# Three weight products as one VectorE instruction over three PSUM banks, two query products as one over two

## The chip, the cores and the metric

The kernel runs on one core of a Trainium2 chip. The metric is the time of one launch in device microseconds (us), the median of several runs. A second figure, the span, is read from one profiled execution: from its first to its last instruction.

## The reference, cut to what matters

One decoder layer over x of 32 x 64 x 512 (2048 rows of 512), in three stages, each followed by a layer norm over 512:

1. x = LN(x + A(x)), with A a small network of four layers on 64 channels (a scan along the sequence and a feed forward of 64 to 256 to 64), projected from 512 and back to 512.
2. x = LN(x + AC(x, ctx, ctx)), the autocorrelation attention. For each of 8 heads and each channel: corr = ifft(fft(q) * conj(fft(k))) over 64 positions, the 8 largest lags, a softmax over them, and a weighted sum of v shifted by these lags (positions clamped to the last one).
3. x = LN(x + FF(x)), with x and weight fake-quantized in blocks of 32 to a 4-bit format, one 512 x 512 product and a bias.

In the kernel the transforms of stage 2 are products with constant matrices. A complex product in the frequency domain is three real products of sums ("forms"), and 96 rows of them hold 32 frequencies of one sequence. The forms of ctx are computed once and kept in SBUF (`ctxf`, three chunks of 512 columns for each tile: sequence 0, sequence 1, and a rest chunk with what is left of both).

## The kernel before, in words

The 2048 rows are 16 tiles of 128 rows (`PAIRS`, each two sequences of 64). All five engines have an instruction stream written out by hand, and semaphores order them. The first part, `slot_loop`, is stage 1. Then comes a software pipeline of 22 turns (`for t in range(1, PAIRS + LAG)`, with LAG = 7) in which every engine works once on up to seven tiles at different stages. One turn of VectorE, in its order (lines 1177 to 1193), for the tile number in brackets: `top_sum` (t-3), `fed` (t-7), `attended` (t), `weight_products` (t-4), `block_scales` (t-5), `without_largest` (t-3), `largest` (t-2), `crossed` (t-4), `rounding` (t-5), `query_products` (t-1).

Those that matter here:

- `query_products` (L1053): two multiplications of 96 partitions x 512, banks 5 and 6 of PSUM (`query_forms`, L376) by `ctxf`, into PQ. `correlation` (L387) on TensorE needs both.
- `weight_products` (L1095): three multiplications of 128 x 512. The first is of bank 7 (`weight_rest_forms`, L411), the other two of banks 5 and 6 (`weight_forms`, L419). TensorE's `out_rest` (L429) reads the first result and `out_even` (L436) the other two.
- Banks 5 and 6 are used in turn by query forms and weight forms: L419 waits until the query products have been read out (`s_pq`), and L376 until the weight products have been (`s_pw`).
- The two matmuls of L419 use 64 rows each, on different halves of the array, and so do those of L376.
- `block_scales` (`scales`, L999 a reduction, L1001 and L1002 tensor_scalar on 128 x 16, L1003 a reciprocal), then `without_largest` (L1083, eight match_replace). L1083 releases GpSimd's `chosen` (L852), which releases TensorE's transposes `weights_to_time` (L401), then ScalarE's copy (L639), then L411 and L419.
- `rounding` (`magic`, L1007 and L1008) releases GpSimd's `clamped` (L858, L859), behind which stand in GpSimd's order `differences` (L841 to L843), `rounded_off` (L865 and the dequantization L754), `finished` (L875) and, in the next turn, `scaled` (L749) and `chosen` (L852).
- TensorE's order in a turn: feed forward (L461, L464), L401, projection (L363), L411, L419, L387, L429, L376, L444, L436.

Of the kernel before, what the change touches and what calls it, by code (L numbers as in the profile page):

```python
# [6 lines left out]
ALU = mybir.AluOpType  # L7
# [8 lines left out]
L = 64  # L16
# [6 lines left out]
PAIRS = ROWS // P  # L23
HC = ROWS // 2
SEQ = HC // L
N = 512
# [9 lines left out]
EVEN = 96  # L36
# [113 lines left out]
def build(nc, xT, x, ctx_in, consts_in, winT, w1T, w2T, woutT, cols, wq_in, rows, out):  # L150
    with ExitStack() as stack:
        def sb(name, shape, dt=F32):
            return stack.enter_context(nc.sbuf_tensor(name, shape, dt))
# [4 lines left out]
        ps = stack.enter_context(nc.psum_tensor("ps", [P, 8 * N], F32))  # L158

        def bank(b):  # L160
            return ps[:, b * N:(b + 1) * N]


        ctxf = sb("ctxf", [P, PAIRS * 3 * N])
# [32 lines left out]
        def piece(k, n=1):  # L197
            return big[:, k * N:(k + n) * N]
# [11 lines left out]
        PQ = piece(0, 2)  # L210
# [1 line left out]
        REST, G, PART, WN, WT = (piece(4 + k) for k in range(5))  # L212
        part = ctxf[0:SPLIT, (3 * PAIRS - 2) * N:(3 * PAIRS - 1) * N].bitcast(BF16)
        bias3 = win_sb[0:SPLIT, :].bitcast(BF16)
        PW = [piece(9 + k) for k in range(3)]
        JUNK = [piece(12), piece(13), PART]

        def mat(k):
            return consts[:, k * P:(k + 1) * P]
# [34 lines left out]
        def row(n):  # L254
            return X[:, bass.ts(n, N)]
# [16 lines left out]
        def here(n):  # L272

            return 0 <= n < PAIRS
# [61 lines left out]
        def _(pe):  # L336
            mm = nc.tensor.matmul
# [6 lines left out]
            for cc in range(2):  # L344
                for g in range(2):
                    pe.wait_ge(s_xt[2 * cc + g], 16)
                for c in range(VC):
                    for g in range(2):
                        last = mm(ps[g * D:(g + 1) * D, cc * N:(cc + 1) * N], win_sb[:, c * D:(c + 1) * D],  # L349
                                  piece(4 * (2 * cc + g) + c), start=(c == 0), stop=(c == VC - 1))  # L350
# [15 lines left out]
            def query_forms(n):  # L366

                if here(n):
                    pe.wait_ge(s_ln[0], n + 1)
                    for b in range(2):  # L370
                        if n >= 3:
                            pe.wait_ge(s_pw, 3 * n - 7 + b)
                        elif n >= 1:
                            pe.wait_ge(s_pq, 2 * n - 1 + b)
                        half = slice(b * L, (b + 1) * L)
                        mm(bank(5 + b)[0:EVEN, :], mat(XQ_A)[half, 0:EVEN], row(n)[half, :], start=True, stop=True  # L376
                           ).then_inc(s_q, 1)

            def correlation(n):

                if here(n):
                    pe.wait_ge(s_pq, 2 * n + 2)
                    if n >= 1:
                        pe.wait_ge(s_ce, n)
                    for j in range(VC):
                        for b in range(2):
                            last = mm(ps[:, 2 * N + j * P + b * L:2 * N + j * P + (b + 1) * L],  # L387
                                      PQ[0:EVEN, b * N + j * P:b * N + (j + 1) * P], mat(IC_E)[0:EVEN, 0:L],
                                      start=True, stop=True)
                    last.then_inc(s_c, 1)  # L390
# [14 lines left out]
            def weight_rest_forms(n):  # L405

                if here(n):
                    pe.wait_ge(s_wte, n + 1)
                    if n >= 1:
                        pe.wait_ge(s_pw, 3 * n - 2)  # L410
                    mm(bank(7), mat(XW_C), WT, start=True, stop=True).then_inc(s_w, 1)  # L411

            def weight_forms(n):

                if here(n):
                    for b in range(2):
                        pe.wait_ge(s_pq, min(2 * n + 5 + b, 2 * PAIRS))
                        half = slice(b * L, (b + 1) * L)
                        mm(bank(5 + b), mat(XW_A)[half, :], WT[half, :], start=True, stop=True).then_inc(s_w, 1)  # L419

            def out_rest(n):

                if here(n):
                    pe.wait_ge(s_pw, 3 * n + 1)
                    if n == 0:
                        pe.wait_ge(s_rs1, SLOTS + 2)
                    if n >= 1:
                        pe.wait_ge(s_sum[1], n)
                    mm(bank(4), mat(OI_C), PW[0], start=True, stop=False, skip_group_check=True)  # L429

            def out_even(n):

                if here(n):
                    for b in range(2):
                        pe.wait_ge(s_pw, 3 * n + 2 + b)
                        last = mm(bank(4)[b * L:(b + 1) * L, :], mat(OI_A)[:, 0:L], PW[1 + b], start=False,  # L436
                                  stop=True, skip_group_check=True)
                    last.then_inc(s_o, 1)

# [28 lines left out]
            def slot(m, l, s, first, second):  # L468
# [32 lines left out]
                for q in range(4):  # L501
                    if second:
                        if q == 0:
                            pe.wait_ge(s_xn2, m)
                        if early and q == 2:
                            query_forms(0)
                        if early and q >= 2:
                            pe.wait_ge(s_act, 4 * m + q - 5)
                        mm(hb[q], w1z[:, q * P:(q + 1) * P], XN[o], start=True, stop=True).then_inc(s_hidmm, 1)  # L509
                context(3)  # L510
                context(4)
                if early:
                    correlation(0)
                    projection(1)
# [13 lines left out]
            for t in range(1, PAIRS + LAG):  # L528
                feed_forward(t - 7)
                weights_to_time(t - 4)  # L530
                if t >= 2:
                    projection(t)
                weight_rest_forms(t - 4)
                weight_forms(t - 4)
                if t >= 3:
                    correlation(t - 2)
                out_rest(t - 4)
                if t >= 2:
                    query_forms(t - 1)
                if t == 1:  # L540
                    pe.wait_ge(s_sq1, SLOTS + 2)
                    mm(bank(4), mat(MEAN), SQ_LAST, start=True, stop=True).then_inc(s_var1, 1)
                quantized_to_channels(t - 6)
                out_even(t - 4)
# [346 lines left out]
        def _(dve):  # L891
            v_ = nc.vector
            tt, ts, stt = v_.tensor_tensor, v_.tensor_scalar, v_.scalar_tensor_tensor
# [151 lines left out]
            def query_products(n):  # L1045

                if here(n):
                    for b in range(2):
                        dve.wait_ge(s_q, 2 * n + b + 1)
                        if n >= 1:  # L1050
                            dve.wait_ge(s_c, n)
                        at = (3 * n + b) * N
                        tt(PQ[0:EVEN, b * N:(b + 1) * N], bank(5 + b)[0:EVEN, :], ctxf[0:EVEN, at:at + N], ALU.mult  # L1053
                           ).then_inc(s_pq, 1)

            def largest(n):

# [29 lines left out]
            def weight_products(n):  # L1087

                if here(n):
                    for b, (to, chunk) in enumerate(((7, 2), (5, 0), (6, 1))):  # L1090
                        dve.wait_ge(s_w, 3 * n + b + 1)
                        if n >= 1:
                            dve.wait_ge(s_o, n)
                        at = (3 * n + chunk) * N
                        tt(PW[b], bank(to), ctxf[:, at:at + N], ALU.mult).then_inc(s_pw, 1)  # L1095

            def block_scales(n):

# [18 lines left out]
            def slot(m, l, s, first, second):  # L1117
# [25 lines left out]
                if early:  # L1143
                    attended(0)
                    query_products(0)
                    largest(0)
# [30 lines left out]
            for t in range(1, PAIRS + LAG):  # L1177
                top_sum(t - 3)
                fed(t - 7)
                attended(t)  # L1180
                weight_products(t - 4)
                block_scales(t - 5)
                without_largest(t - 3)
                if t >= 3:
                    largest(t - 2)
                crossed(t - 4)
                rounding(t - 5)
                if t == 1:
                    dve.wait_ge(s_mlp, SLOTS)
                    ts(H[:, N:2 * N], XC[1], curm[:, B2:B2 + 1], None, ALU.add).then_inc(s_h, 1)  # L1190
                    last_norm(1, RS_LAST)
                if t >= 2:
                    query_products(t - 1)
# [42 lines left out]
```

## Time and profile before

| | us |
|---|---|
| median of 3 runs | 364.13 (363.85 to 365.54) |
| the profiled execution's own time | 364.46 |
| its span | 362.5 |
| VectorE busy | 274.7 (76%) |
| TensorE busy | 295.6 (82%) |
| GpSimd busy | 184.3 (51%) |
| L1095, weight products, 48 instructions | 30.7 |
| L1053, query products, 32 instructions | 20.5 |

The turns of the pipeline lie between about 151 and 360 us of the span. Each engine's busy time is a mean over the whole span, so a share says little on which of them sets the length of a turn. Of a matmul the end is modelled. In the timeline instructions of one line that follow each other are merged: "x3" and 1.88 us are three instructions from the start of the first to the end of the last.

### The profile page before, as it was taken

The numbers are of one execution on the slowest core, as the hardware profiler recorded it, in microseconds if no ns is written. First come the engines' busy times: TensorE is split into PE (matmuls) and PEld (weight loads), VectorE is DVE, ScalarE is ACT, GpSimd is POOL, SyncE is SP. The second block draws the span as 40 slices with busy tenths as digits, with TensorE's granted clock in tenths as the row PEclk, the third lists the DMA queues.
The fourth block names the chain that finished last, engine by engine and source line by source line (L and its number), as shares of the span: only waits on it lengthen the run. The fifth ranks groups of instructions, "written<-read, shape, count | busy, mean of one in ns | idle before, by whom it ended". The sixth has DMA issues, their size and how long they took to land.

```text
span 362.5 us, 4947 instructions
## 1 busy us (share of the span) xinstructions
PE 295.6 (82%) x1071; PEld 122.9 (34%) x1080; DVE 274.7 (76%) x927; ACT 252.0 (70%) x586; POOL 184.3 (51%) x213
## 2 busy tenths in 40 slices
PE   1578589889899898796599999999999998986633
PEld 1222233333333333241344444433444443332100
DVE  6748695967768578514659999999999999987730
ACT  4028288888988888676647788777879777664722
POOL 1008961041040113100333888888898888988782
PEclk9987699999999999989889999999999999998955
DMA  6999049731021100540000000000000000000002
GB/s 210 393 309 361 32 80 181 146 102 29 0 72 29 29 14 0 155 78 0 1 0 2 2 1 1 31 30 29 32 30 28 5 30 29 31 30 29 30 29 87
DMA packets 14413, 24.53 MB, mean 68 GB/s; under 512 B 2611, under 2 KB 3251, under 8 KB 14390
## 3 DMA queue, kind: packets, MB, share of 16 engines
q1 hardware_dynamic: 12310, 20.09, 16.6%
q0 software_dynamic: 2080, 4.19, 6.9%
q8 instruction: 7, 0.11, 0.1%
q14 instruction: 16, 0.13, 0.1%
HBM read 15.89 MB, written 4.19 MB: 55 GB/s over the span
## 4 chain that ended last, share of the span: by engine, by line
PE 34%; DVE 30%; issue 12%; ACT 10%; POOL 9%; DMA 3%; SPq 1%; POOLq 0%; ACTq 0%; DVEq 0%
PE ps L509 8%; PE ps L477 6%; DVE X L1018 4%; DVE big L1083 4%; PE ps L522 4%; DVE big L1095 3%; DVE m L1064 3%; DMA big<-in_xT_dram 3%; PE ps L349 3%; DVE qa L1001 2%; PE ps L487 2%; DVE qa L999 2%; PE ps L411 2%; PE ps L387 2%; DVE big L1141 2%
## 5 line engine op out<-in xcount | busy, mean ns | idle before, releaser
L749 POOL TENSOR_TENSOR big<-X,qs 128x512 f32<-128x512 f32 x20 | 20.9, 1046 | 60.0 <-DVE qs L1003 59.9
L477 PE MATMUL ps<-ctx_ring,consts 128*128 128x512 f32 x96 | 50.1, 635 | 0.8 <-ACT ctxf L660 0.8
L570 ACT ACTIVATE big<-X,lnv 128x512 f32<-128x512 f32 x48 | 34.2, 712 | 9.6 <-DVE X L1018 9.6
L509 PE MATMUL ps<-big,w1z 128*128 128x512 f32 x64 | 31.4, 632 | 10.9 <-DVE big L1141 10.0
L1018 DVE SCALAR_TENSOR_TENSOR X<-ps,X 128x512 f32<-128x512 f32 x48 | 31.9, 679 | 10.8 <-PE ps L464 7.2
L1095 DVE TENSOR_TENSOR big<-ps,ctxf 128x512 f32<-128x512 f32 x48 | 30.7, 681 | 5.4 <-PE ps L411 3.7
L387 PEld LDWEIGHTS ps<-consts,big 96*128 96x128 f32 x256 | 29.9, 191 | 12.0 <-issue 11.1
L387 PE MATMUL ps<-consts,big 96*128 96x64 f32 x256 | 31.9, 278 | 0.1
L477 PEld LDWEIGHTS ps<-ctx_ring,consts 128*128 128x128 f32 x96 | 18.0, 200 | 30.2 <-ACT ctxf L660 15.8
L692 ACT ACTIVATE big<-ps,curm 128x512 f32<-128x512 f32 x32 | 22.0, 692 | 6.7 <-PE ps L509 6.7
L852 POOL TENSOR_TENSOR big<-big 128x512 f32<-128x512 f32 x16 | 20.3, 1269 | 11.7 <-DVE big L1083 11.6
L599 ACT ACTIVATE X<-X,lnv 128x512 f32<-128x512 f32 x32 | 24.7, 807 | 2.0
L1083 DVE MATCH_REPLACE8 big<-w,big 128x64 f32<-128x64 f32 x128 | 25.0, 208 | 0.1
L660 ACT ACTIVATE ctxf<-ps 128x512 f32 (+1 forms) x40 | 23.3, 594 | 0.7 <-PE ps L477 0.6
L1053 DVE TENSOR_TENSOR big<-ps,ctxf 96x512 f32<-96x512 f32 x32 | 20.5, 679 | 4.1 <-PE ps L376 4.1
L761 POOL TENSOR_SCALAR big<-big 128x512 f32<-128x512 f32 x4 | 2.5, 613 | 41.1 <-issue 41.0
L509 PEld LDWEIGHTS ps<-big,w1z 128*128 128x128 f32 x64 | 11.7, 194 | 29.8 <-issue 21.0
L754 POOL TENSOR_TENSOR xq<-big,qs 128x512 bf16<-128x512 f32 x20 | 21.0, 1050 | 1.6
L859 POOL TENSOR_TENSOR big<-big 128x512 f32<-128x512 f32 x16 | 20.3, 1268 | 1.3
L411 PE MATMUL ps<-big,consts 128*128 128x512 f32 x32 | 18.7, 667 | 2.7 <-ACT big L639 2.7
L1064 DVE MAX8 m<-big 128x8 f32<-128x64 f32 x128 | 17.6, 210 | 3.8 <-ACT big L608 3.8
L865 POOL TENSOR_TENSOR big<-big 128x512 f32<-128x512 f32 x16 | 20.4, 1272 | 0.2
(175 smaller groups left out, 695.9 us busy)
## 6 DMA issues: line engine op xcount, KB each, us to landing
big<-in_xT_dram SPq DMA_DIRECT2D x4, 1024.0 KB, 10.9
ctx_ring<-in_ctx_dram SPq DMA_DIRECT2D x16, 256.0 KB, 2.8
out_dram<-X SPq DMA_DIRECT2D x16, 256.0 KB, 2.0
X<-in_x_dram SPq DMA_DIRECT2D x2, 1536.0 KB, 12.7
X<-rows_sb POOLq DMA_DIRECT2D x1, 3072.0 KB, 22.0
X<-in_wq_dram SPq DMA_DIRECT2D x1, 1024.0 KB, 8.2
X<-in_x_dram SPq DMA_DIRECT2D x2, 512.0 KB, 4.0
X<-rows_sb POOLq DMA_DIRECT2D x1, 1024.0 KB, 8.0
```

The costliest lines, as they stand in the source:

```text
L387: last = mm(ps[:, 2 * N + j * P + b * L:2 * N + j * P + (b + 1) * L], PQ[0:EVEN, b * N + j * P:b * N + (j + 1) * P], mat(IC_E)[0:EVEN, 0:L ...
L411: mm(bank(7), mat(XW_C), WT, start=True, stop=True).then_inc(s_w, 1)
L477: mm(bank(6 + t % 2), mat((CY_0, CY_1, CY_C)[t % 3]), ctx_ring[:, r * N:(r + 1) * N], start=True, stop=True).then_inc(s_cform, 1)
L509: mm(hb[q], w1z[:, q * P:(q + 1) * P], XN[o], start=True, stop=True).then_inc(s_hidmm, 1)
L570: squared[k] = chain(a(JUNK[k], row(n), ACT.Square, bias=st[:, 0:1], scale=-float(V), accum_out=st[:, 2:3]))
L599: a(row(n), row(n), ACT.Identity, bias=st[:, 5:6], scale=st[:, 4:5]).then_inc(s_ln[k], 1)
L660: a(ctxf[:, bass.ts(6 * m + t, N)], bank(6 + t % 2), ACT.Copy).then_inc(s_fe, 1)
L692: a(hs[q], hb[q], ACT.Silu, bias=curm[:, B1_0 + q % 2:B1_0 + q % 2 + 1]).then_inc(s_act, 1)
L1018: stt(row(m), bank(b), 0.0, row(m), ALU.add, ALU.add, accum_out=st[:, 0:1]).then_inc(s_sum[k], 1)
L1064: last = v_.max(top[:, g * TOP:(g + 1) * TOP], CR[n % 2][:, g * L:(g + 1) * L])
L1083: last = v_.match_replace(REST[:, g * L:(g + 1) * L], w8[:, g * TOP:(g + 1) * TOP], G[:, g * L:(g + 1) * L], 0.0)
L1095: tt(PW[b], bank(to), ctxf[:, at:at + N], ALU.mult).then_inc(s_pw, 1)
```

## The change: what it does

The three multiplications become one of 128 x 1536 over banks 5, 6 and 7, the two become one of 96 x 1024 over banks 5 and 6. Results lie in the same SBUF columns, those of the rest chunk now last. Each of these instructions increments its semaphore once, so all waits on `s_pw` and `s_pq` count tiles and no longer pieces. The weight product now waits for all three forms (`s_w` at 3n+3), the query product for both (`s_q` at 2n+2). TensorE's waits follow: one for the whole product in place of one for each piece.

```diff
 def query_forms(n):
     pe.wait_ge(s_ln[0], n + 1)
+    if n >= 3:
+        pe.wait_ge(s_pw, n - 2)
+    elif n >= 1:
+        pe.wait_ge(s_pq, n)
     for b in range(2):
-        if n >= 3:
-            pe.wait_ge(s_pw, 3 * n - 7 + b)
-        elif n >= 1:
-            pe.wait_ge(s_pq, 2 * n - 1 + b)
...
 def correlation(n):
-    pe.wait_ge(s_pq, 2 * n + 2)
+    pe.wait_ge(s_pq, n + 1)
...
 def weight_rest_forms(n):
-    pe.wait_ge(s_pw, 3 * n - 2)
+    pe.wait_ge(s_pw, n)
...
 def weight_forms(n):
+    pe.wait_ge(s_pq, min(n + 3, PAIRS))
     for b in range(2):
-        pe.wait_ge(s_pq, min(2 * n + 5 + b, 2 * PAIRS))
...
 def out_rest(n):
-    pe.wait_ge(s_pw, 3 * n + 1)
+    pe.wait_ge(s_pw, n + 1)
-    mm(bank(4), mat(OI_C), PW[0], start=True, stop=False, skip_group_check=True)
+    mm(bank(4), mat(OI_C), piece(PW + 2), start=True, stop=False, skip_group_check=True)
...
 def out_even(n):
     for b in range(2):
-        pe.wait_ge(s_pw, 3 * n + 2 + b)
...
 def query_products(n):
-    for b in range(2):
-        dve.wait_ge(s_q, 2 * n + b + 1)
-        if n >= 1:
-            dve.wait_ge(s_c, n)
-        at = (3 * n + b) * N
-        tt(PQ[0:EVEN, b * N:(b + 1) * N], bank(5 + b)[0:EVEN, :], ctxf[0:EVEN, at:at + N], ALU.mult
-           ).then_inc(s_pq, 1)
+    dve.wait_ge(s_q, 2 * n + 2)
+    if n >= 1:
+        dve.wait_ge(s_c, n)
+    tt(PQ[0:EVEN, :], ps[0:EVEN, 5 * N:7 * N], ctxf[0:EVEN, 3 * n * N:(3 * n + 2) * N], ALU.mult
+       ).then_inc(s_pq, 1)
...
 def weight_products(n):
-    for b, (to, chunk) in enumerate(((7, 2), (5, 0), (6, 1))):
-        dve.wait_ge(s_w, 3 * n + b + 1)
-        if n >= 1:
-            dve.wait_ge(s_o, n)
-        at = (3 * n + chunk) * N
-        tt(PW[b], bank(to), ctxf[:, at:at + N], ALU.mult).then_inc(s_pw, 1)
+    dve.wait_ge(s_w, 3 * n + 3)
+    if n >= 1:
+        dve.wait_ge(s_o, n)
+    tt(piece(PW, 3), ps[:, 5 * N:8 * N], ctxf[:, 3 * n * N:3 * (n + 1) * N], ALU.mult
+       ).then_inc(s_pw, 1)
```

## Rows read from the trace of the kernel before

**Rows 1.** The page, busy us of each engine, share of the span, instructions.

```profile
PE 295.6 (82%) x1071; PEld 122.9 (34%) x1080; DVE 274.7 (76%) x927; ACT 252.0 (70%) x586; POOL 184.3 (51%) x213
```

**Rows 2.** Busy time in four stretches of one turn each, from 222.90 to 264.60.

```profile
sum 41.70, PE 39.78 PEld 17.80 DVE 41.15 ACT 33.89 POOL 35.66; mean PE 9.95 PEld 4.45 DVE 10.29 ACT 8.47 POOL 8.92
```

**Rows 3.** Timeline of a full turn: start, us, engine, line, count, idle time before.

```profile
261.70 0.43 DVE L1008 TENSOR_SCALAR big<-big 128x512 f32<-128x512 f32 x1
...
262.05 1.28 DVE L1053 TENSOR_TENSOR big<-ps,ctxf 96x512 f32<-96x512 f32 x2
...
263.52 1.13 PE L419 MATMUL ps<-big,consts 64*128 64x512 f32 x4
...
264.59 1.88 DVE L1095 TENSOR_TENSOR big<-ps,ctxf 128x512 f32<-128x512 f32 x3
...
266.39 0.67 DVE L999 TENSOR_REDUCE qa<-X 128x16 f32<-128x512 f32 x1
...
267.02 1.05 POOL L754 TENSOR_TENSOR xq<-big,qs 128x512 bf16<-128x512 f32 x1
267.09 1.01 DVE L1001 TENSOR_SCALAR qa<-qa 128x16 int32<-128x16 int32 x1
...
268.13 0.20 DVE L1002 TENSOR_SCALAR qs<-qa 128x16 f32<-128x16 f32 x1
```

**Rows 4.** Line 1001 over the whole span: ns min/median/max, first and last start.

```profile
L1001 DVE TENSOR_SCALAR qa<-qa x20: 174/390/1023, 27.5 to 343.9; 128x16 int32<-128x16 int32 x20
```

**Rows 5.** Groups of the page; and a timeline row with eight short VectorE instructions.

```profile
L1095 DVE TENSOR_TENSOR big<-ps,ctxf 128x512 f32<-128x512 f32 x48 | 30.7, 681 | 5.4 <-PE ps L411 3.7
...
L1053 DVE TENSOR_TENSOR big<-ps,ctxf 96x512 f32<-96x512 f32 x32 | 20.5, 679 | 4.1 <-PE ps L376 4.1
...
270.20 1.10 DVE L1064 MAX8 m<-big 128x8 f32<-128x64 f32 x8
```

**Rows 6.** Timeline of the first turns with weight products, 184 to 207 us.

```profile
188.83 1.27 POOL L852 TENSOR_TENSOR big<-big 128x512 f32<-128x512 f32 x1 [5.05 <-DVE big L1083]
...
190.69 0.66 PE L401 MATMUL ps<-consts,big 128*128 128x128 f32 x4
...
193.09 1.13 PE L419 MATMUL ps<-big,consts 64*128 64x512 f32 x4
...
194.25 1.29 DVE L1095 TENSOR_TENSOR big<-ps,ctxf 128x512 f32<-128x512 f32 x2 [0.21 <-PE ps L419]
...
196.38 0.17 DVE L1002 TENSOR_SCALAR qs<-qa 128x16 f32<-128x16 f32 x1
...
198.41 1.27 POOL L852 TENSOR_TENSOR big<-big 128x512 f32<-128x512 f32 x1 [0.45 <-DVE big L1083]
...
202.14 1.13 PE L419 MATMUL ps<-big,consts 64*128 64x512 f32 x4
...
202.60 1.99 DVE L1095 TENSOR_TENSOR big<-ps,ctxf 128x512 f32<-128x512 f32 x3
...
205.21 0.39 DVE L1001 TENSOR_SCALAR qa<-qa 128x16 int32<-128x16 int32 x1
...
205.64 0.17 DVE L1002 TENSOR_SCALAR qs<-qa 128x16 f32<-128x16 f32 x1
205.66 1.07 POOL L754 TENSOR_TENSOR xq<-big,qs 128x512 bf16<-128x512 f32 x1
```

**Rows 7.** Timeline of the last turns with weight products, 308 to 339 us.

```profile
308.84 0.18 DVE L1002 TENSOR_SCALAR qs<-qa 128x16 f32<-128x16 f32 x1
308.85 1.07 POOL L754 TENSOR_TENSOR xq<-big,qs 128x512 bf16<-128x512 f32 x1
...
311.65 1.26 POOL L852 TENSOR_TENSOR big<-big 128x512 f32<-128x512 f32 x1
...
316.52 1.29 DVE L1095 TENSOR_TENSOR big<-ps,ctxf 128x512 f32<-128x512 f32 x2 [0.34 <-PE ps L419]
...
337.23 1.29 DVE L1095 TENSOR_TENSOR big<-ps,ctxf 128x512 f32<-128x512 f32 x2 [0.36 <-PE ps L419]
```

More of the change, by code:

```diff
@@ L214, in build @@
         bias3 = win_sb[0:SPLIT, :].bitcast(BF16)
-        PW = [piece(9 + k) for k in range(3)]
+        PW = 9
         JUNK = [piece(12), piece(13), PART]
@@ L434, in out_even @@
                     for b in range(2):
-                        pe.wait_ge(s_pw, 3 * n + 2 + b)
-                        last = mm(bank(4)[b * L:(b + 1) * L, :], mat(OI_A)[:, 0:L], PW[1 + b], start=False,
+                        last = mm(bank(4)[b * L:(b + 1) * L, :], mat(OI_A)[:, 0:L], piece(PW + b), start=False,
                                   stop=True, skip_group_check=True)
```

## The prediction

> **What bounds the kernel now.** I read the page's busy shares first, then the busy time of single turns, then the timeline of one full turn, and last the timelines of the first and the last turns that have weight products. The page shows no engine full over the span [rows 1]. Four turns in the middle take 41.70 us, 10.42 each, and in them VectorE is busy 41.15 of 41.70, TensorE 39.78, GpSimd 35.66 [rows 2]. So VectorE looks like the bound there, and fewer instructions on it look like time won.
>
> The timeline of one turn says otherwise [rows 3]. L1001 works on 16 columns, and its shortest instances take 0.174 us [rows 4]. In this turn it takes 1.01: from 267.09 to 268.10, where GpSimd's L754, begun at 267.02, ends at 268.07. In the eight turns from 215 to 299 us I see the same: L754 starts 0.05 to 0.07 before L1001, and L1001 ends about 0.03 after it. Where VectorE came first, L1001 or L1002 took 0.17 to 0.39, as at 205.21 and 205.64 [rows 6]. So 0.8 us of VectorE's busy time in a full turn is waiting for GpSimd, and the turn is a loop of both: L1008 ends, GpSimd runs L858 to L754, L1001 ends 0.03 behind L754, then VectorE runs L1002, L1083, L1064 and so on to the next L1008. From the end of L1008 (262.13) to the end of L1001 (268.10) are 5.97 us, and the weight products lie inside these beside GpSimd's work [rows 3]. While L1001 loses that race, no saving in the products shortens a turn.
>
> **The price of an instruction.** Three products take 1.88 us with 0.68 for the last alone, a step of 0.60 [rows 3, 5]. Eight L1064 of 64 elements take 1.10 with 0.21 for the last, a step of 0.127 [rows 5]. A line through both gives 1.06 ns an element and 0.06 us an instruction. The trace has no instruction over several banks. The bounds of the fixed part are 0 (three products still cost 1.80) and 0.127 (a whole short instruction; they cost 1.55). A step from bank to bank could cost something too, but nothing in rows prices it. I take 0.06, since it accounts for both steps: the weight product 1.68 instead of 1.80, the query product 1.14 instead of 1.20. Over 16 tiles these are 16 x 0.18 = 2.9 us of VectorE time.
>
> The Trainium skill ("Perfetto Trace Analysis", Optimizing Scalar/DVE Operations) gives a larger estimate, about 125 ns of data access per VectorE instruction from PSUM, and advises larger operations for a saturated engine. By it the weight product saves 0.25 us a turn, not 0.12. The same section advises the reverse, breaking up instructions, where an engine is not saturated and others wait for it, and that is the case of the first and last turns below.
>
> **What the merged wait costs.** The merged product needs both L419 forms. The two matmuls run side by side, so waiting for the second costs nothing; what is lost is the first product (bank 7), which now waits as well. A product that waited for L419 started 1.16 after it: 193.09 to 194.25 [rows 6]. In a full turn that is 263.52 + 1.16 = 264.68, where before the first one started at 264.59. The merged one ends its step at 264.68 + 1.68 = 266.36, against 266.39. L1001 is then ready at 267.06, 0.03 earlier than before, but L754 starts at 267.02 as ever [rows 3]: it still loses, by 0.04. The query product ends near 263.2 and L419 starts at 263.52 behind L411, so that wait stays covered. TensorE's L429 and L376 now wait for all products (about 266.45); L429 follows L387 at about the same time, and TensorE has 10.42 - 9.95 = 0.47 us free in a turn [rows 2]. So the full turns stay at 10.42: term 0.
>
> **The first turns.** Here VectorE waits for L419 and the first product was ahead of it. The weight products then end 1.68 instead of 1.21 (two steps of 0.60) after the release: +0.47 us a turn. Turn by turn:
> - The turn at 185 us: L852 moves from 188.83 to 189.30 and ends at 190.57; L401 starts at 190.69 behind other matmuls [rows 6]. Hidden.
> - The turn at 194: +0.47, and L852 at 198.41 had waited for L1083, so it, L401 and L419 at 202.14 move by 0.47 [rows 6].
> - The turn at 203: L419 at 202.61, product from 203.77 to 205.45, L1001 ready at 206.16. L754, which hangs on L1008 and so moves by 0.47 as well, starts at 206.13. Before, L1001 and L1002 got in ahead of it (205.21, 205.64). Now L1001 loses by 0.03, ends at 206.13 + 1.05 + 0.03 = 207.21, and L1002 starts at 207.24 instead of 205.64: +1.60 [rows 6].
> The loop then carries 1.60 through the full turns.
>
> **The last turns.**
> - At 308, where before L1002 (308.84) got in ahead of L754 (308.85), the same geometry makes L1001 lose: L1002 at 309.96, 1.12 later. From L1002 to L852 are 2.03 (196.38 to 198.41), so L852 comes at 311.99; before, it stood at 311.65, not waiting for VectorE: +0.34 [rows 6, 7].
> - At 316.52 the products waited for L419: +0.47 again, 0.81 in all [rows 7].
> - At 326 the delay is largely hidden, since the chain goes through GpSimd. At 337.23 it is +0.47: 1.28 in all [rows 7].
>
> Sum: 1.60 + 0 + 1.28 = 2.9 us. Against the profiled execution's own time, 364.46 (span 362.5), that is 367.4; this execution is 0.33 over the median of the runs, so 367.0 for the median. If the delays of both ends are half covered, it is 365.6. With the product at 1.80, L1001 loses by more and each edge turn pays 0.12 more, some 0.5 in all: 367.5. With 1.55, L1001 is ready at 266.93, ahead of L754, which is the first rival.
>
> **Rivals.**
> 1. *The race is won.* L1001 gets in ahead of L754 at 205, in full turns and at 308. A win gives VectorE 0.8 us, but TensorE's chain L401 to L419 does not follow at once, so I expect a win in every second turn, about 0.4 a turn, with TensorE's 0.47 as the cap. Nine turns give 3.5 us; the edges still cost 0.47 three or four times, 1.7. Time 364.1 - 3.5 + 1.7 = 362.3. For it: the margin is only 0.04 and the true step may be 1.60 to 1.65. Against it: L1001 lost at 0.05 late, and L1002 won only when it started ahead (205.64 against 205.66). Chance 0.16. By the page's 125 ns the margin would turn to 0.09 in favour.
> 2. *VectorE is the plain bound* and the waits are covered: the 2.9 us are won, 361.2. For it: 10.29 busy of 10.42. Against it: L1001's 1.01. Chance 0.08.
> 3. *The edges absorb it.* The full turns gain nothing, and most of the delays of the first and last turns fall beside GpSimd or TensorE work: 364.1 to 365.9. For it: the turn at 185 and the one at 326 hide theirs. Chance 0.22.
> 4. *The product over banks is slower than three* (over 1.80), or TensorE starves behind the late L429: beyond 368.3. Chance 0.06.
> The forecast itself has 0.48, with its own range of 366.0 to 368.3.
>
> **How the numbers follow.** A measurement of this kernel tells about 0.5% from no change, 1.8 us: faster is below 362.3, slower above 365.95. Slower: 0.48 + 0.06 + a little of rival 3, 0.56. Faster: half of rival 1 and rival 2, with what lies near the edge, 0.16. Same: 0.28. The range leaves out rival 2 and the upper tail and reaches into rival 1: 362.4 to 368.3.
>
> **What would show each step.** In the profile after: a weight product of about 1.75 us (step 1.68) that starts 1.16 after L419 in every turn, with idle VectorE ahead of it in full turns too; the full turn still 10.42; L1001 at 1.01 in all full turns, and now also at the two places near 206 and 309. The forecast is wrong if L1001 is short in the full turns (rival 1), if the full turn falls to about 10.2 with VectorE unbroken (rival 2), or if L419 of the turn at 212 us is late by much less than 1.6 (rival 3).

## The result and the profile after

The changed kernel takes 369.24 us (median of 4 runs, 367.99 to 370.39), the kernel before 364.84 beside it (4 runs). The ratio is 1.0118, with a 95% interval of 1.0064 to 1.0172: slower, by about 4.4 us. I had forecast 367.0 within 362.4 to 368.3, a loss of 2.9 us. The direction was right, the loss was forecast 1.5 us too small, and the time lies outside the range. Measured once more in six runs the ratio was 1.0154 (1.0118 to 1.0190), 5.6 us between the medians. Executions more than 1.5% over the fastest of their kernel stay out of the ratios: two of the twelve with the query products alone (366.03 and 366.92), and one of the kernel before (382.93).

The two profiled executions differ by 3.5 us in span (362.5 and 366.0), but the changed one happened to reach the pipeline 1.6 us sooner: the first L851, which was L852 before, starts at 177.38 against 178.96. (The page's lines have shifted by up to five: L1090 is now the weight product, L1050 the query product, L1000 and L1001 the two tensor_scalar, L1007 was L1008, L753, L851, L864 and L874 were L754, L852, L865 and L875.) The next fences are timeline rows (start, us, engine, line, count, idle time before), first of the changed kernel: the first, fourth and thirteenth L851, the last one, and the last L874.

```profile
177.38 1.27 POOL L851 TENSOR_TENSOR big<-big 128x512 f32<-128x512 f32 x1 [2.65 <-DVE big L1080]
...
208.00 1.27 POOL L851 TENSOR_TENSOR big<-big 128x512 f32<-128x512 f32 x1 [0.38 <-DVE big L1080]
...
301.81 1.27 POOL L851 TENSOR_TENSOR big<-big 128x512 f32<-128x512 f32 x1 [0.36 <-DVE big L1080]
...
333.07 1.27 POOL L851 TENSOR_TENSOR big<-big 128x512 f32<-128x512 f32 x1 [0.36 <-DVE big L1080]
...
362.81 0.77 POOL L874 TENSOR_SCALAR X<-X,lnv 128x512 f32<-128x512 f32 x1 [2.98 <-ACT lnv L578]
```

The same instructions before:

```profile
178.96 1.27 POOL L852 TENSOR_TENSOR big<-big 128x512 f32<-128x512 f32 x1 [2.65 <-DVE big L1083]
...
207.81 1.27 POOL L852 TENSOR_TENSOR big<-big 128x512 f32<-128x512 f32 x1
...
301.62 1.27 POOL L852 TENSOR_TENSOR big<-big 128x512 f32<-128x512 f32 x1 [0.36 <-DVE big L1083]
...
331.53 1.26 POOL L852 TENSOR_TENSOR big<-big 128x512 f32<-128x512 f32 x1
...
359.30 0.77 POOL L875 TENSOR_SCALAR X<-X,lnv 128x512 f32<-128x512 f32 x1 [2.99 <-ACT lnv L579]
```

With this instruction as a clock for the turns, the pipeline divides as follows (starts read from the traces, us):

| stretch | before | changed | difference |
|---|---|---|---|
| first three turns (first to fourth L851) | 28.85 | 30.62 | +1.77 |
| nine full turns | 93.81 | 93.81 | 0.00 |
| next three turns | 29.91 | 31.26 | +1.35 |
| from the last L851 to the last L874 | 27.77 | 29.74 | +1.97 |
| sum | 180.34 | 185.43 | +5.09 |

These are single profiles, and two entries look more exact than they are. The full turns come out equal partly by luck: before, one took 10.57 and one 10.33, the others 10.41 to 10.42, and in the changed kernel they take 10.40 to 10.43. The first of the first three turns took 9.87 before, but 9.35 in the profiles of two kernels below (late release, moved line), where TensorE's granted clock is 0.50 for a shorter stretch around it (178.4 to 181.6 with the late release, 178.1 to 184.7 before, 176.2 to 182.8 in the changed kernel). So a stretch outside the full turns is sure to about 0.5 us, an estimate from these two values.

One full turn of the changed kernel, which answers to [rows 3]:

```profile
262.00 0.43 DVE L1007 TENSOR_SCALAR big<-big 128x512 f32<-128x512 f32 x1
262.35 1.21 DVE L1050 TENSOR_TENSOR big<-ps,ctxf 96x1024 f32<-96x1024 f32 x1
...
263.81 1.13 PE L419 MATMUL ps<-big,consts 64*128 64x512 f32 x4
265.01 1.76 DVE L1090 TENSOR_TENSOR big<-ps,ctxf 128x1536 f32<-128x1536 f32 x1
...
266.69 0.68 DVE L998 TENSOR_REDUCE qa<-X 128x16 f32<-128x512 f32 x1
...
267.33 1.05 POOL L753 TENSOR_TENSOR xq<-big,qs 128x512 bf16<-128x512 f32 x1
267.40 1.01 DVE L1000 TENSOR_SCALAR qa<-qa 128x16 int32<-128x16 int32 x1
268.44 0.20 DVE L1001 TENSOR_SCALAR qs<-qa 128x16 f32<-128x16 f32 x1
```

The reader is to see three things. The product's step is 265.01 to 266.69, 1.68 us. It starts 1.20 after L419, not 1.07 as the first of three did. And L1000 is still 0.07 behind L753 and blocked to its end. At the first turn with a full load, around 205 us, the race that was won before is now lost [rows 6]:

```profile
204.85 1.05 POOL L753 TENSOR_TENSOR xq<-big,qs 128x512 bf16<-128x512 f32 x1
204.91 1.02 DVE L1000 TENSOR_SCALAR qa<-qa 128x16 int32<-128x16 int32 x1
205.96 0.17 DVE L1001 TENSOR_SCALAR qs<-qa 128x16 f32<-128x16 f32 x1
```

In the last turn the wait for the whole product leaves TensorE idle, and then it is slow. First L429 of that turn before, then the changed kernel, where 337.23 and its neighbours stood in [rows 7]:

```profile
337.13 1.12 PE L429 MATMUL ps<-big,consts 128*128 128x512 f32 x2
```

```profile
338.07 1.76 DVE L1090 TENSOR_TENSOR big<-ps,ctxf 128x1536 f32<-128x1536 f32 x1 [2.38 <-PE ps L419]
...
339.88 2.06 PE L429 MATMUL ps<-big,consts 128*128 128x512 f32 x2 [1.89 <-DVE big L1090]
...
342.30 1.57 PE L435 MATMUL ps<-big,consts 128*64 128x512 f32 x4
...
343.93 0.69 DVE L1017 SCALAR_TENSOR_TENSOR X<-ps,X 128x512 f32<-128x512 f32 x1 [2.80 <-PE ps L435]
```

L429 took 1.12 before, beside the second product, and now takes 2.06 behind it. In the stretch 340.0 to 343.4 the granted clock is 0.51, that is the 1.2 GHz level. The view gives the stretch's length, busy time and count of each engine, then the clock and DMA:

```profile
340.00:343.40 3.40, 3.40 (x10) 1.18 (x10) 1.02 (x4) 0.96 (x3) 1.42 (x2) 0.51 0.20 77
```

One turn earlier it is the same: L429 waits 1.89 us and takes 1.82, and the clock is 0.50 from 329.8 to 333.0.

### The profile page after: what moved, and what is told of

Same layout as the page of the kernel before. It is cut to its first block, busy times and chain, and to the rows that moved or that the text cites. A ratio compares the mean times of both kernels' runs of the same rounds, so it can differ in the third digit from the quotient of the medians.

```text
span 366.0 us, 4854 instructions
## 1 busy us (share of the span) xinstructions
PE 297.1 (81%) x1071; PEld 122.9 (34%) x1080; DVE 273.3 (75%) x879; ACT 252.5 (69%) x586; POOL 184.0 (50%) x213
## 4 chain that ended last, share of the span: by engine, by line
PE 37%; DVE 19%; POOL 18%; issue 11%; ACT 10%; DMA 4%; SPq 1%; POOLq 0%; ACTq 0%; DVEq 0%
PE ps L508 8%; PE ps L476 6%; DMA big<-in_xT_dram 4%; PE ps L521 4%; POOL big L851 3%; PE ps L419 3%; PE ps L411 3%; POOL big L748 3%; POOL big L858 2%; POOL big L864 2%; PE ps L486 2%; PE ps L363 2%; DVE big L1080 2%; DVE qa L1000 2%; POOL big L842 2%
## 5 line engine op out<-in xcount | busy, mean ns | idle before, releaser
L476 PE MATMUL ps<-ctx_ring,consts 128*128 128x512 f32 x96 | 48.1, 610 | 2.1 <-ACT ctxf L659 2.1
L1017 DVE SCALAR_TENSOR_TENSOR X<-ps,X 128x512 f32<-128x512 f32 x48 | 32.0, 680 | 13.1 <-PE ps L463 7.2
L1090 DVE TENSOR_TENSOR big<-ps,ctxf 128x1536 f32<-128x1536 f32 x16 | 28.1, 1758 | 10.4 <-PE ps L419 9.3
L851 POOL TENSOR_TENSOR big<-big 128x512 f32<-128x512 f32 x16 | 20.3, 1271 | 13.5 <-DVE big L1080 13.5
L476 PEld LDWEIGHTS ps<-ctx_ring,consts 128*128 128x128 f32 x96 | 17.1, 192 | 29.8 <-ACT ctxf L659 16.3
L429 PE MATMUL ps<-big,consts 128*128 128x512 f32 x32 | 19.6, 698 | 3.8 <-DVE big L1090 3.8
L1050 DVE TENSOR_TENSOR big<-ps,ctxf 96x1024 f32<-96x1024 f32 x16 | 19.4, 1213 | 4.1 <-PE ps L376 4.1
L753 POOL TENSOR_TENSOR xq<-big,qs 128x512 bf16<-128x512 f32 x20 | 21.0, 1049 | 1.6
L411 PE MATMUL ps<-big,consts 128*128 128x512 f32 x32 | 18.6, 664 | 2.7 <-ACT big L638 2.7
L864 POOL TENSOR_TENSOR big<-big 128x512 f32<-128x512 f32 x16 | 20.4, 1278 | 0.2
```

The costliest lines, as they stand in the source:

```text
L476: mm(bank(6 + t % 2), mat((CY_0, CY_1, CY_C)[t % 3]), ctx_ring[:, r * N:(r + 1) * N], start=True, stop=True).then_inc(s_cform, 1)
L851: g_.tensor_tensor(WN, G, REST, ALU.subtract).then_inc(s_wn, 1)
L864: chain.then_wait(g_.tensor_tensor(VB, VB, MB, ALU.subtract))
L1017: stt(row(m), bank(b), 0.0, row(m), ALU.add, ALU.add, accum_out=st[:, 0:1]).then_inc(s_sum[k], 1)
L1090: tt(piece(PW, 3), ps[:, 5 * N:8 * N], ctxf[:, 3 * n * N:3 * (n + 1) * N], ALU.mult).then_inc(s_pw, 1)
```

## The experiments

Theory A is that of the prediction: GpSimd and VectorE form a loop that sets the full turn, and the loss lies in the first and last turns. B is that an instruction over several banks is costly by itself, C that the query product's release costs. All ratios are to the kernel before on the same chip, with 95% intervals. "Pipeline" is the time from the first L852 to the last L875 (180.34 before, 185.43 changed), as the profile has it.

### Query products alone

```diff
 weight products and their waits as in the kernel before
+tt(PQ[0:EVEN, :], ps[0:EVEN, 5 * N:7 * N], ctxf[0:EVEN, 3 * n * N:(3 * n + 2) * N], ALU.mult).then_inc(s_pq, 1)
```

> Only the two query products are merged; the weight products are as before. Theory A (a full turn is the loop L1008, GpSimd to L754, L1001; the loss of the change lies in the first and last turns, in the weight product's late start and late release): no loss, ratio to before 0.990 to 1.001. VectorE comes 0.07 us earlier to L1001, which puts it level with L754 (before: 0.07 late), so single turns may be won. Theory B (an instruction over several banks is itself what costs): slower, by a share of the 1.2% of the change. Theory C (the query product's single release makes L419 or L376 wait): slower, L419 more than 1.05 us after L411.

Measured 0.9962 (0.9934 to 0.9989), pipeline 180.18. The full turn fell from 10.42 to 10.21. Here are L852, the two tensor_scalar and the next L852:

```profile
256.50 1.27 POOL L852 TENSOR_TENSOR big<-big 128x512 f32<-128x512 f32 x1
...
263.74 0.17 DVE L1001 TENSOR_SCALAR qa<-qa 128x16 int32<-128x16 int32 x1
263.75 1.07 POOL L754 TENSOR_TENSOR xq<-big,qs 128x512 bf16<-128x512 f32 x1
...
263.95 0.90 DVE L1002 TENSOR_SCALAR qs<-qa 128x16 f32<-128x16 f32 x1
...
266.71 1.27 POOL L852 TENSOR_TENSOR big<-big 128x512 f32<-128x512 f32 x1
```

0.07 us decided it: L1001 starts 0.01 ahead of L754 and takes 0.17. But L754 then runs when L1002 starts, 0.21 after L1001, and L1002 takes 0.90 instead. So winning once gains 0.2 a turn, not 0.8.

The nine full turns gain 1.47 us (92.34 against 93.81), and yet the pipeline gains only 0.16: behind the last L852 stand 29.09 us instead of 27.77. TensorE has the half clock there from 325.4 to 332.0, where the kernel before has it only from 331.7 to 334.9 (in the view's columns named above):

```profile
325.40:332.00 6.60, 5.70 (x17) 2.06 (x17) 3.17 (x17) 1.57 (x5) 5.16 (x7) 0.50 0.10 40
```

The weight products and L429 wait here as before, so a fall of the clock at this place does not need the merged product. B and C are out as far as the query merge goes.

### Weight products alone

```diff
 query products and their waits as in the kernel before
+tt(piece(PW, 3), ps[:, 5 * N:8 * N], ctxf[:, 3 * n * N:3 * (n + 1) * N], ALU.mult).then_inc(s_pw, 1)
```

> Only the weight products are merged; the query products are two as before. Theory A: the whole loss is here: full turns 10.42 with L1001 at 1.0, ratio 1.009 to 1.015, and a little over the change's own time, since 0.07 us of VectorE's time in a turn is missing in the first and last turns. Theory C (query merge carries a share): clearly under the change's ratio.

Measured 1.0159 (1.0124 to 1.0193), pipeline 185.40, beside 1.0154 and 185.71 of the changed kernel on the same chip. The two cannot be told apart: the whole loss is in the weight merge.

### The rest product alone again

```diff
-dve.wait_ge(s_w, 3 * n + 3)
-tt(piece(PW, 3), ps[:, 5 * N:8 * N], ctxf[:, 3 * n * N:3 * (n + 1) * N], ALU.mult).then_inc(s_pw, 1)
+dve.wait_ge(s_w, 3 * n + 1)
+tt(piece(PW + 2), bank(7), ctxf[:, (3 * n + 2) * N:3 * (n + 1) * N], ALU.mult).then_inc(s_pw, 1)
+dve.wait_ge(s_w, 3 * n + 3)
+tt(piece(PW, 2), ps[:, 5 * N:7 * N], ctxf[:, 3 * n * N:(3 * n + 2) * N], ALU.mult).then_inc(s_pw, 1)
```

> The rest product (bank 7) is its own instruction again, first in order, waits for its own form and releases the out_rest matmul by itself; the other two are one instruction over two banks, and the query product is one. Theory A: the 0.6 us of late start and the late release are gone, VectorE reaches L1001 about 0.13 us earlier than before, ahead of L754 by 0.06, so it wins in some full turns: ratio 0.990 to 0.999, short instances of that tensor_scalar (0.2 to 0.4 us) among the full turns. Theory B: still slower than before, 1.003 or more, since it has two instructions over banks in a turn. If the race is lost as before: 0.999 to 1.001.

Measured 0.9990 (0.9966 to 1.0014), pipeline 180.15, full turn 10.18. L1001 starts 0.06 ahead of L754 and takes 0.17, and L1002 is blocked for 0.93. The full turns gain 1.74 us (92.07 against 93.81), and the stretch behind the last L852 loses 1.30 (29.07), with the clock at 0.50 from 325.6 to 332.3 as with the query products alone. The loss of the change is gone with two merged instructions still in each turn, so B is out: merging the two products that become ready together costs nothing, merging the one that is ready earlier does.

### Late start alone

```diff
-dve.wait_ge(s_w, 3 * n + b + 1)
+dve.wait_ge(s_w, 3 * n + 3)
```

> The kernel before, with one edit: each of the three weight products waits for all three forms, so the first (bank 7) starts late; they stay three instructions and are released one by one. Theory A: full turns stay at 10.42 us with L1001 at 1.01; each first and last turn ends its products 0.6 us later, the race is lost at about 205 and 308 us too; the last turn's L429 is released after the first product, so the last 2 us of the change's loss are missing: 2.5 to 3.5 us over before, ratio 1.006 to 1.010. Theory B: no loss, 0.999 to 1.001, since no instruction spans banks.

Measured 1.0057 (1.0026 to 1.0088), pipeline 182.85, 2.5 over before. Three single instructions lose too, if the first has to wait. Of the 2.5 us, 1.2 lie in the first three turns (30.07) and 1.3 in the three before the last L852 (31.25, the changed kernel 31.26); behind it are 27.60, none of the changed kernel's loss. The full turn is 10.42 again, although L1001 is now 0.20 late:

```profile
266.72 1.05 POOL L754 TENSOR_TENSOR xq<-big,qs 128x512 bf16<-128x512 f32 x1
266.92 0.88 DVE L1001 TENSOR_SCALAR qa<-qa 128x16 int32<-128x16 int32 x1
```

Later by 0.13, blocked for 0.13 less: L1001's end is L754's end, whenever VectorE arrives.

### Late release alone

```diff
 def out_rest(n):
-    pe.wait_ge(s_pw, 3 * n + 1)
+    pe.wait_ge(s_pw, 3 * n + 3)
```

> The kernel before, with one edit: the out_rest matmul (L429) waits for all three weight products instead of the first. Theory A: the full turns don't change (L429 follows L387 anyway), in the last turn L429 and so L436 and the residual behind it come 1.4 to 2 us later, partly at the half clock: 1 to 2.2 us over before, ratio 1.003 to 1.006. Theory B and C: no change, 0.999 to 1.001.

Measured 0.9973 (0.9947 to 0.9999), pipeline 179.51. Theory A had said 1 to 2.2 us slower, and this is not slower. The rows show L429 and L436:

```profile
334.54 1.13 PE L429 MATMUL ps<-big,consts 128*128 128x512 f32 x2 [1.37 <-DVE big L1095]
...
335.81 1.08 PE L436 MATMUL ps<-big,consts 128*64 128x512 f32 x4
```

L429 waited as intended, but it and L436 take 1.13 and 1.08, so they ran at the full clock. The residual behind L436 (L1018) starts 8.62 us after the last L852, against 8.21 before, but the next residual 10.04 after it, against 10.32: the delay is gone there. Behind the last L852 this kernel takes 27.50 us; the kernel before takes 27.77, with a half-clock stretch at its last L401. The late release by itself is nearly free. My theory for the last 2 us had failed. The next two experiments test another one, the clock.

### The changed kernel once more

No edit.

> The changed kernel once more, for a second profile of its last turns. From the first of L852 to the last L875 the first profile took 5.1 us more than before: 1.8 in the first three steps from L852 to L852, 0 in the nine full ones, 1.35 in the last three, 2.0 behind them. If the half clock of TensorE behind its idle 1.9 us in the last turn belongs to the change, this profile has it too, and the stretch behind the last L852 is 29 to 30 us again. If it was chance: 27.5 to 28.5. Ratio 1.008 to 1.015.

Measured 1.0154 (1.0118 to 1.0190), pipeline 185.71, of it 29.91 behind the last L851. L429 again waits 1.89 and 1.88 us in the last two turns, and the clock is 0.50 from 331.9 to 335.1 and from 342.1 to 345.3, behind the same two waits. It was not chance.

### TensorE kept busy in the last two turns

```diff
+if t - 4 >= PAIRS - 2 and here(t - 4):
+    pe.wait_ge(s_sum[0], PAIRS)
+    mm(bank(0), mat(IDENT), consts[:, 0:N], start=True, stop=True)
+    mm(ps[:, 0:N // 2], mat(IDENT), consts[:, 0:N // 2], start=True, stop=True)
 out_rest(t - 4)
```

> The changed kernel; in the last two turns with weight products TensorE does two matmuls more ahead of out_rest (L429), of constants into bank 0, which nothing reads (512 and 256 columns, about 1.6 us), in the 1.8 us in which it otherwise waits for the merged product. If the half clock in these two turns comes of that idle time, it is gone, and the stretch from the last L852 to the last L875 falls from 29.8 to about 28, 1.5 to 2.5 us off the changed kernel in all: ratio to before 1.006 to 1.011. If the late release alone costs these 2 us: no change, 1.012 to 1.016.

Measured 1.0090 (1.0061 to 1.0119), pipeline 183.69: behind the last L852 28.03 instead of 29.74. This kernel has more work than the changed one and is faster. Its ratio stands beside 1.0154 from another chip; in the profiles it is 1.74 us less from the first L852 to the last L875. In the same stretch as above, and with L1094 as the weight product:

```profile
340.00:343.40 3.40, 3.16 (x14) 1.20 (x15) 2.13 (x8) 0.98 (x3) 1.86 (x3) 1.00 0.23 82
```

```profile
340.24 1.12 PE L429 MATMUL ps<-big,consts 128*128 128x512 f32 x2 [0.40 <-DVE big L1094]
```

The clock stays at 1.00 and L429 takes 1.12 instead of 2.06. Of the 1.97 us behind the last L852, 1.7 are gone with the half clock.

### GpSimd's L754 halved in the changed kernel

The pipeline's dequantization leaves out columns 256 to 511.

```diff
+w = NBLK // 2 if which else NBLK
-g_.tensor_tensor(blocks(xq[:, :]), blocks(VB), ...
+g_.tensor_tensor(blocks(xq[:, 0:w * BLK]), blocks(VB[:, 0:w * BLK]), ...
```

> The changed kernel, but GpSimd's L754 multiplies only the first 256 of 512 columns in the last part (half of the dequantization is left out). VectorE, ScalarE and TensorE have all their work. Theory A: the loop L1008, GpSimd, L1001 is 0.5 us shorter: L1001 0.5 to 0.6 instead of 1.0, full turn 9.9 to 10.1 instead of 10.42, 4 to 7 us under the changed kernel, ratio to before 0.993 to 1.004. Rival (the merged product's wait for L419, or VectorE's work, sets the turn): still 10.42 and 1.009 to 1.016.

Measured 0.9901 (0.9875 to 0.9928), pipeline 177.18. (Lines are shifted again: L853 is the changed kernel's L851, L754 its L753, L1002 its L1000.)

```profile
239.10 1.27 POOL L853 TENSOR_TENSOR big<-big 128x512 f32<-128x512 f32 x1 [0.37 <-DVE big L1082]
...
246.34 0.61 POOL L754 TENSOR_TENSOR xq<-big,qs 128x256 bf16<-128x256 f32 x1
246.43 0.55 DVE L1002 TENSOR_SCALAR qa<-qa 128x16 int32<-128x16 int32 x1
...
249.09 1.27 POOL L853 TENSOR_TENSOR big<-big 128x512 f32<-128x512 f32 x1 [0.37 <-DVE big L1082]
```

0.44 off L754 (1.05 to 0.61) takes 0.43 off the turn (10.42 to 9.99), with all of VectorE's and TensorE's work and the merged product in place. That is the loop.

The whole gain is larger than forecast: 8.3 us of pipeline under the changed kernel instead of 4 to 7. The nine full turns give 3.98 of it, the three behind them 1.31, the first three 0.38, and 2.58 lie behind the last L853 (27.16 instead of 29.74). There the clock did not fall. L429 waits 1.89 us for the merged product in both last turns, as in the changed kernel, and takes 1.13 and 1.12:

```profile
325.72 1.13 PE L429 MATMUL ps<-big,consts 128*128 128x512 f32 x2 [1.89 <-DVE big L1092]
...
335.69 1.12 PE L429 MATMUL ps<-big,consts 128*128 128x512 f32 x2 [1.89 <-DVE big L1092]
```

```profile
325.00:341.50 16.50, 10.29 (x40) 3.35 (x40) 11.56 (x38) 9.67 (x30) 12.07 (x13) 1.00 0.09 33
```

So the idle 1.89 us alone does not bring the clock down, and at the full clock the merged wait costs nothing behind the last turn's L853.

### fed moved in VectorE's turn: on the kernel before, on the change, and with merges

```diff
 top_sum(t - 3)
-fed(t - 7)
 attended(t)
 weight_products(t - 4)
 block_scales(t - 5)
+fed(t - 7)
 without_largest(t - 3)
```

> The kernel before, with one line moved in VectorE's turn: fed(t-7) stands behind block_scales(t-5) instead of ahead of attended(t). No product is merged. VectorE reaches L1001 0.61 us earlier, while GpSimd is still in L865, so L1001 and L1002 both get in ahead of L754, as they did at 205 us. Theory A (the race sets the full turn): L1001 at 0.2 to 0.6, L1002 at 0.17, the full turn 10.0 to 10.2, 2 to 4 us under before, ratio 0.989 to 0.995. Rival (VectorE's sum of work is the bound): the same work in another order, turn 10.42, ratio 0.999 to 1.001.

Measured 0.9901 (0.9876 to 0.9927), 359.35 us, pipeline 176.67, with no product merged. L1001 arrives during L865 and both tensor_scalar get in:

```profile
245.78 1.26 POOL L852 TENSOR_TENSOR big<-big 128x512 f32<-128x512 f32 x1
...
251.59 1.28 POOL L865 TENSOR_TENSOR big<-big 128x512 f32<-128x512 f32 x1
252.58 0.32 DVE L1001 TENSOR_SCALAR qa<-qa 128x16 int32<-128x16 int32 x1
252.93 0.17 DVE L1002 TENSOR_SCALAR qs<-qa 128x16 f32<-128x16 f32 x1
252.94 1.07 POOL L754 TENSOR_TENSOR xq<-big,qs 128x512 bf16<-128x512 f32 x1
...
255.75 1.27 POOL L852 TENSOR_TENSOR big<-big 128x512 f32<-128x512 f32 x1
```

The turn is 9.97. The same line moved in the changed kernel:

> The changed kernel with the same line moved. Theory A: the merged product waits for L419 in any case, so freeing VectorE ahead of it brings L1001 no earlier, and fed now stands behind it: L1001 still 0.03 to 0.07 us behind L754 at 1.0 us, full turn 10.42, ratio to before 1.008 to 1.016. Rival (it is VectorE's order of work that costs, not the wait for L419): the full turn falls as in the kernel before with the line moved, ratio under 1.003.

Measured 1.0311 (1.0273 to 1.0349), pipeline 194.16. L1000 loses as expected (it takes 1.00 to 1.02 behind L753), but the turn is 11.04, not 10.42: I had overlooked that behind L1001 `fed` stands on the loop itself, and adds its 0.61. With the race lost the move costs 0.6 a turn, with it won it gains 0.45. With the rest product alone and the merges of two banks:

> Both: the rest product alone and first, the other two merged over two banks, the query product merged, and fed(t-7) behind block_scales. Theory A: L1001 and L1002 are short in every full turn, as with the moved line alone (turn 9.96 there). The merges take up to 0.13 us off VectorE's part ahead of L1001, which now waits for L865 anyway, so the turn stays 9.9 to 10.0: ratio 0.987 to 0.993. Rival (VectorE's sum of work is the bound): 0.2 us a turn more than the moved line alone, ratio 0.982 to 0.986.

Measured 0.9914 (0.9883 to 0.9944), turn 9.97. With the query merge only:

> The query products merged, the weight products three as before, fed(t-7) behind block_scales. Theory A: as the moved line alone, turn 9.9 to 10.0, ratio 0.987 to 0.992, within 0.3% of it. Rival (VectorE's sum of work is the bound): 0.07 us a turn less than that.

Measured 0.9917 (0.9891 to 0.9944), turn 9.97. The three cannot be told apart: once both short instructions are ahead of L754, fewer instructions on VectorE are worth nothing that I can measure. What sets the turn of 9.97 is not tested. All three beat the kernel before and the changed one; the plainest is the single moved line.

## Why the prediction was wrong in size: right on the full turns, wrong on the last turns

- **The price of an instruction** was right: step 1.68 forecast, 1.68 measured (265.01 to 266.69); for the query product a step of 1.14 forecast and 1.13 measured (it starts at 262.35 and takes 1.21, the next instruction of VectorE starts at 263.48). The Trainium skill ("Perfetto Trace Analysis", Optimizing Scalar/DVE Operations) would have had 0.25 us saved by merging three; the trace shows 0.12. Its other advice there, to break up instructions where others wait for them, is what the rest product alone again bears out (0.9990 against 1.0154).
- **The full turns** stayed at 10.42, term 0: right, and shown to be the loop by halving L754. The product started 1.20 after L419, I had 1.16, so the margin of the race was 0.07, not 0.04. The Trainium skill ("SBUF — State Buffer", Who interferes with whom) says that of a VectorE instruction in a two-port mode and one of GpSimd the second to start is blocked until the first ends. The traces agree where L1001 starts second: at +0.20 and +0.07 it is blocked to the end of L754, at -0.01 it is not. They do not show it the other way round: L754, begun 0.01 behind L1001 of 0.17 us, takes 1.07 instead of 1.05. No trace shows the mode that L1001 runs in.
- **The first turns**: 1.60 forecast, 1.77 measured up to the fourth L851. Counted from the first L851, L401 in the turn at 185 starts only 0.07 later than before, hidden as forecast; by the L851 that ends the turn at 194 the delay is 0.76, where I had 0.47; and the race at 205 was lost as forecast.
- **The last turns** are the step that failed. For the three turns ahead of the last L852 I had 0.34 + 0.47 = 0.81 and found 1.35. I had L1001 lose only at 308; it loses in all three (1.00 to 1.01 us at 309, 319 and 330), and each of them stays a full 10.42, where the kernel before had 10.03, 9.85 and 10.03. These are the races at 319 and 330, first before, then changed:

```profile
318.44 0.17 DVE L1001 TENSOR_SCALAR qa<-qa 128x16 int32<-128x16 int32 x1
...
328.30 0.39 DVE L1001 TENSOR_SCALAR qa<-qa 128x16 int32<-128x16 int32 x1
```

```profile
319.54 1.00 DVE L1000 TENSOR_SCALAR qa<-qa 128x16 int32<-128x16 int32 x1
...
329.96 1.01 DVE L1000 TENSOR_SCALAR qa<-qa 128x16 int32<-128x16 int32 x1
```

The clock has no part in this: the kept-busy kernel has the same 155.7 us up to the last L852. Behind the last L852 I had 0.47 (the turn at 326 hidden, +0.47 at 337) and found 1.97. I had priced when VectorE ends its product and not what TensorE does meanwhile: it stands idle for 1.89 us, then runs at 1.2 GHz, and L429, L435 and the residual behind them (L1017) are late. The fourth rival had named TensorE behind the late L429, at a chance of 0.06; the forecast itself held nothing for it. Keeping it busy took back 1.7 of the 1.97. That the late release is cheap at the full clock is shown by three of the experiments: 27.50 behind the last L852 with it, 27.60 without it (the late start), and 27.16 with the merged product itself and L754 halved.
- **The size of the first rival** was off. I gave a won race 0.4 us a turn. In full turns a win by L1001 alone is worth 0.2, since L1002 takes its place; only both together give 0.45.

Sum: 2.9 forecast, 5.09 in the pipeline of the profile, and 4.4 between the medians, 5.6 in the second measurement. Open stays what brings the clock down. It fell behind 1.89 us of idle time in the changed kernel, but not behind the same 1.89 us with L754 halved, nor behind the 1.37 us of the late release; and it fell for longer than before in two kernels without the merged wait (29.09 and 29.07 behind the last L852). What is shown is that filling the idle time kept it up in the changed kernel. How much of the 1.97 us belongs to the change is therefore uncertain: it is measured against one profile of the kernel before.

## What to carry to other kernels

Before saving instructions on an engine that looks full, look for one whose duration changes from place to place with the same shape: its busy time is a wait, and the work ahead of it may be free. Merge what becomes ready at the same moment; whatever was ready earlier pays the wait, and every consumer of it as well, and this shows in the first and last turns of a pipeline, where nothing covers it. Where a change shifts TensorE's idle time there, look at the granted clock in the profile after: here it was up to 2 us, and the length of the idle time alone did not foretell it.

## What the runs showed of the hardware that I had not expected

- A race between VectorE and GpSimd is decided within 0.07 us, and VectorE, where it loses, takes up to 1.02 us for an instruction of 0.17. After L1001 wins, L1002 starts 0.21 later behind L754 and takes 0.90: one win does not protect the next instruction.
- A VectorE multiplication over three PSUM banks takes 1.758 us, over two 1.21: as one over 512 columns plus 0.54 for each further bank. No cost of crossing a bank shows (two banks over 96 partitions, three over 128).
- Two matmuls more in each of the last two turns with products, whose results nothing reads, made the changed kernel faster: 1.0090 where it had 1.0154 on another chip, 1.74 us in the profiles. The granted clock stayed at 1.00 through these turns.
- TensorE idle for 1.89 us twice was followed by the half clock in the changed kernel (two profiles) and with the weight products alone, and not with L754 halved (clock 1.00 from 325.0 to 341.5).
